# Causal attention of a four-layer kernel: heads taken in pairs, fp32 products in four groups of 32 columns, keys read from a DRAM scratch

## The chip, the cores and the metric

The kernel runs on one core of a Trainium2 chip. Its engines work side by side: TensorE (PE, with its weight loads as PEld), VectorE (DVE), ScalarE (ACT), GpSimd (POOL) and SyncE (SP), which here only issues DMAs. The metric is the device time of one launch in microseconds (us), the median of several runs.

## What is computed

The reference runs four layers, each a gated attention-like block and a gated feed-forward block, on x of 4 x 512 x 512. The change touches one block alone, the attention of layer 3: the queries are the normalised x, keys and values are both ctx_2048 (4 x 512 x 512), 16 heads of 32 columns, causal.

```python
qh = q.reshape(B, Sq, HEADS, hd).transpose(0, 2, 1, 3)      # B 4, Sq 512, HEADS 16, hd 32
scores = jnp.einsum('bhqd,bhkd->bhqk', qh, kh) / math.sqrt(hd)
scores = jnp.where(causal[None, None], scores, jnp.asarray(MASKED_BIAS, scores.dtype))
attn = jax.nn.softmax(scores, axis=-1)
out = jnp.einsum('bhqk,bhkd->bhqd', attn, vh)
...
x = x + jnp.tanh(g_xattn[3]) * _L3_xattn_ref(_layernorm(x, axis=-1), ctx_2048, ctx_2048)
```

## The kernel before

The whole program is a chain of stages with a barrier after each; only `layer3_xattn` (L2593) and its `attention_causal` (L2053) are touched. Two stages of it matter. `transposed_parts` (L174) normalises x, splits it into a high and a low fp16 part and turns both into `qT`; in this one use its SP queue also reads the same two parts of the context from a DRAM scratch, `context_parts`, into `kT` (L122, L123).

`attention_causal` then works on 64 items, one for each of 16 heads and 4 batches. N is 2048 = 4 batches of S = 512 rows, P = 128, KT = 4. An item has these steps:

- **Loading.** SP copies, head by head, six slices of 128 KB from `qT` and `kT` into `qs` and `ks` (L2103, L2104): the two fp16 parts stacked in 3 x 32 = 96 rows, so that one product gives a score from split operands.
- **Tops** (`score_for_top`, L2165, L2167). For 128, 256, 384 and 512 keys TensorE makes the scores of 128 queries each, and adds a causal mask by a second product; DVE takes the maximum of each (L2310) and splits the negated maximum into two fp16 numbers (L2314, L2316).
- **The turn of the shift.** TensorE turns those (L2176), ACT copies them out (L2256), and SP sends them by two DMAs into rows 96 and 97 of `qs` (L2117). In `ks` these rows hold the number 1024, and rows 98 to 127 of both were cleared by DVE at the start (L2354 to L2357), so that the second score product, over all 128 rows, comes out already less its maximum.
- **Scores and exponentials** (L2185, L2186, L2264), transposed: keys on partitions, 512, 384, 256 and 128 queries wide; ACT takes the exponential of three pieces.
- **Mix** (L2195). Four fp32 products of 64 columns (32 of the head's values, 32 ones, in `hv`, which POOL fills at L2138) with 512, 384, 256 and 128 moving columns give the numerator and the sums in one bank, `mixed_at`.
- **Evacuation.** DVE copies the sums (L2321), then ACT the numerator (L2272), and only then may the next mix begin. DVE inverts a 128 x 128 piece per item (L2324), POOL multiplies once a head (L2145), TensorE turns the head's output (L2202) and DVE adds it to x in four instructions (L2338).

Each engine's order is written out by hand. On TensorE one item is: tops of the item four further on, scores of the next item, mix of this item, turn of the shift. Loops of four heads on PE and two on ACT and DVE carry heads 2 to 13.

`attention_clipped` (L1497), the attention of layer 2, is not touched; it is named because it contains fp32 products of 32 columns (L1566, L1569) in four groups.

## Time and profile before

| | |
|---|---|
| Median of 3 runs | 4006.91 us (4003.19 to 4008.08) |
| The profiled execution | 4001.78 us, its span 4000.0 us |
| Engines busy in the span | PE 3024.1 us (76%), DVE 2748.0 (69%), ACT 1869.0 (47%), POOL 736.7 (18%) |
| Mean granted TensorE clock | 0.879 of full |

The profile is one execution: every time below is taken from it, with 0 at its first instruction. Shares of the whole span say little here, since the stages have different limits; `attention_causal` occupies the stretch from 3569.9 us to 3892.4 us. Matmuls are pipelined: a record runs on past the start of the next, so what a product costs is read from start to start. An fp32 product leaves two records, one for each of its passes, and a timeline row merges records that follow each other.

### The profile page before, as it was taken

How to read it: one execution, taken by the hardware profiler on the slowest of the kernel's cores; microseconds unless marked ns; L12 is line 12 of the kernel's file. 1: busy time of each engine (PE TensorE's matmuls, PEld its weight loads, DVE VectorE, ACT ScalarE, POOL GpSimd, SP SyncE). 2: the span in 40 equal slices, each digit the busy share in tenths (PEclk: the TensorE clock that was granted, in tenths of full speed). 3: DMA queues.
4: the chain of work that ended last, by engine and by line, in shares of the span. 5: the costliest groups of instructions: out<-in, count | busy, mean ns of one | idle time of the engine just before them, and what ended most of it. 6: DMA issues, size and time to landing. Idle time of an engine off the chain costs nothing. (4 is left out here: it accounts for less than half of the span.)

```text
span 4000.0 us, 66664 instructions
## 1 busy us (share of the span) xinstructions
PE 3024.1 (76%) x21656; PEld 1554.8 (39%) x21656; DVE 2748.0 (69%) x4984; ACT 1869.0 (47%) x2753; POOL 736.7 (18%) x595
## 2 busy tenths in 40 slices
PE   4999579977679999999965477867885137749972
PEld 2444334433346556565643233332112113225541
DVE  4322542326689999999965666443996877988877
ACT  2222422223259999999973333314770112425531
POOL 4222020001210000000022133120115002540102
PEclk9999679999789999999987688878997559969996
DMA  3000300010000000000003000102310200032201
GB/s 126 11 0 0 126 1 0 0 55 11 14 16 11 12 11 6 11 11 11 1 11 129 11 0 0 53 14 61 77 43 19 84 0 0 0 108 49 46 21 45
DMA packets 52277, 120.49 MB, mean 30 GB/s; under 512 B 11312, under 2 KB 14384, under 8 KB 50224
## 3 DMA queue, kind: packets, MB, share of 16 engines
q1 hardware_dynamic: 52144, 118.67, 10.0%
q8 instruction: 90, 1.47, 0.2%
q14 instruction: 43, 0.35, 0.0%
HBM read 72.37 MB, written 8.39 MB: 20 GB/s over the span
## 5 line engine op out<-in xcount | busy, mean ns | idle before, releaser
L1044 DVE TENSOR_REDUCE s_top<-ps 128x1 f32<-128x512 f32 x1024 | 657.0, 683 | 32.4 <-PE ps L939 32.0
L1013 ACT ACTIVATE s_prob<-ps,s_shift,m_sq 128x1024 int16<-128x1024 f32 x512 | 615.2, 1202 | 30.8 <-DVE s_shift L1052 30.8
L939 PE MATMUL ps<-s_ks,s_qs 128*128 128x512 f16 x1024 | 352.0, 386 | 61.6 <-issue 15.6
L944 PEld LDWEIGHTS ps<-ident,s_prob 128*128 128x128 f16 x4096 | 272.9, 98 | 123.5 <-DVE m_o L1062 51.7
L944 PE MATMUL ps<-ident,s_prob 128*128 128x128 f16 x4096 | 314.5, 220 | 0.7 <-ACT s_prob L1013 0.5
L932 PE MATMUL ps<-s_ks,s_qs 128*128 128x512 f16 x1024 | 307.3, 382 | 1.0 <-ACT s_prob L1013 0.5
L242 PE MATMUL ps<-ident,s_parts 128*128 128x128 f16 x1024 | 126.2, 300 | 217.2 <-POOL s_parts L233 214.7
L1019 ACT ACTIVATE s_probT<-ps 128x1024 f16<-128x1024 int16 x256 | 262.1, 1024 | 6.8 <-PE ps L944 6.3
L604 DVE SCALAR_TENSOR_TENSOR s_prod<-ps,scale,s_silu 128x512 f32<-128x512 f32 x64 | 48.0, 750 | 230.1 <-ACT s_silu L588 230.1
L376 DVE TENSOR_TENSOR s_prod<-ps,s_masked 128x512 f32<-128x512 f32 x64 | 44.3, 692 | 218.6 <-POOL s_masked L352 218.6
L242 PEld LDWEIGHTS ps<-ident,s_parts 128*128 128x128 f16 x1024 | 93.9, 136 | 251.8 <-POOL s_parts L233 251.8
L222 ACT ACTIVATE s_parts<-s_rows 128x512 f16<-128x512 f32 x112 | 69.4, 628 | 248.4 <-DVE s_rows L253 190.0
L317 PE MATMUL ps<-m_cT,s_hid 128*128 128x512 f16 x768 | 175.6, 379 | 9.6 <-DVE s_hid L371 9.6
L305 PE MATMUL ps<-m_hT,m_cT 128*128 x768 | 177.7, 383 | 1.9 <-PEq L104 1.9
L1057 DVE CAST s_probT<-ps 128x1024 f16<-128x1024 int16 x256 | 174.2, 681 | 3.2 <-PE ps L944 3.2
L1643 DVE TENSOR_SCALAR s_prob<-ps,s_cap 128x1024 f32<-128x1024 f32 x128 | 158.1, 1269 | 24.9 <-PE ps L1552 24.9
L588 ACT ACTIVATE s_silu<-ps,scale 128x512 f32<-128x512 f32 x64 | 44.0, 687 | 258.3 <-PE ps L556 258.3
L233 POOL TENSOR_TENSOR s_parts<-s_rows,s_parts 128x512 f16<-128x512 f32 x112 | 137.4, 1259 | 116.5 <-ACT s_parts L222 116.5
L1587 ACT ACTIVATE s_prob<-s_prob 128x1024 f32<-128x1024 f32 x128 | 131.1, 1051 | 58.3 <-DVE s_prob L1643 55.3
L923 POOL TENSOR_TENSOR s_sums<-s_z 128x16 f32<-128x16 f32 x16 | 3.5, 217 | 835.9 <-DVE m_o L1062 835.9
L340 ACT ACTIVATE s_silu<-ps 128x512 f32<-128x512 f32 x64 | 38.1, 596 | 249.2 <-PE ps L305 249.2
L2195 PE MATMUL ps<-s_prob,s_hv 128*64 128x512 f32 (+3 forms) x512 | 152.0, 440 | 3.0 <-ACT s_num L2272 2.9
(301 smaller groups left out, 6522.2 us busy)
## 6 DMA issues: line engine op xcount, KB each, us to landing
s_qs<-m_qT SPq DMA_DIRECT2D x144, 128.0 KB, 2.4
s_ks<-m_kT SPq DMA_DIRECT2D x144, 128.0 KB, 2.4
x_sb<-in_x SPq DMA_DIRECT2D x1, 4096.0 KB
s_rows<-in_ctx SPq DMA_DIRECT2D x16, 256.0 KB, 2.9
context_parts<-m_cT SPq DMA_DIRECT2D x1, 4096.0 KB, 17.2
m_nat<-in_L_ffn_W_up SPq DMA_DIRECT2D x4, 1024.0 KB, 9.6
m_nat<-in_L_ffn_W_gate SPq DMA_DIRECT2D x4, 1024.0 KB
m_nat<-in_L_ffn_W_down SPq DMA_DIRECT2D x4, 1024.0 KB, 6.6
```

The lines of the kernel that those rows point to most:

```text
L242: t = pe.transpose(k.ps16[:, u, cols(m, P)], parts[:, u, m // DC, cols(m % DC, P)], k.ident[:])
L305: i = pe.matmul(k.ps[:, n % A, :], cT[:, lw, c, e * D + f * P:e * D + (f + 1) * P], hT[:, lx, c, bass.ds(g * GT, GT)], start=(m == c == 0) ...
L317: i = pe.matmul(k.ps[:, YB + t, :], hid[:, n % Q, lh, cols(t, P)], cT[:, lw, f, cols(e, D)], start=(n == m == 0), stop=(n == UNITS - 1 and ...
L932: j = pe.matmul(pair(half)[:, m, :], qs[:, hb, bass.ds(t * P, P)], ks[:, hb, cols(2 * half + m, 512)], start=True, stop=True)
L939: pe.matmul(quarter_at(q), qs[:, hb, bass.ds(t * P, P)], ks[:, hb, cols(q, 512)], start=True, stop=True).then_inc(s.top_scored, 1)
L944: j = pe.transpose(turned(half, F16)[:, cols(m, P)], prob[:, u, cols(8 * half + m, P)].bitcast(F16), k.ident[:])
L1013: act.activation(prob[:, u, cols(half, HALF)], pair(half).rearrange("p m n -> p (m n)"), ACT.Exp, bias=shift[:, u:u + 1], scale=sq[:, bass ...
L1019: act.activation(probT[:, u, 8:16, :].rearrange("p m n -> p (m n)"), turned(1, I16), ACT.Copy).then_inc(s.half1_copied, 1)
L1044: dve.tensor_reduce(top4[:, u, q:q + 1], quarter_at(q), AX.X, ALU.max).then_inc(s.top_read, 1)
L1057: dve.tensor_copy(probT[:, u, 0:8, :].rearrange("p m n -> p (m n)"), turned(0, I16)).then_inc(s.half0_copied, 1)
L1643: dve.tensor_scalar(prob[:, n % R, :, :], k.ps[:, 2 * (n % A):2 * (n % A) + 2, :], cap[:, tile:tile + 1], -LIMIT, ALU.min, ALU.max).then_i ...
L2195: j = pe.matmul(mixed_at[0:2 * HD, t * P:S], hv[:, a, b * KT + t, :], prob[:, b % 2, START[t]:START[t] + S - t * P], start=(t == 0), stop= ...
```

## The change

`attention_causal` is rewritten for items of a pair of heads and a batch: 32 items instead of 64. What it does, with line numbers of the changed file:

- **Keys** come straight from the scratch into `ks`, 512 KB per DMA for four heads, three DMAs for each group of four heads (L2116). `kT` and the two reads in `transposed_parts` are gone. `ks` has eight head slots instead of four, `qs` four pairs. Queries still come from `qT`, in 128 KB DMAs whose pieces are now 1 KB long (L2110).
- **98 rows.** The score product contracts 98 rows, the tops 96 as before, so nothing is cleared. The rows of 1024 are written as fp32 words of two, in two instructions of 2 x 4096 (L2337, L2342).
- **Tops** of a pair: the same products and maxima for each head, the widest first; the two splitting instructions, the turn, the copy and the DMA of the shift are once for the pair. The turn goes to a spare part of bank 1.
- **Scores** use three banks in rotation, six pieces for an item.
- **Mix** (L2205): for each key tile four fp32 products of 32 columns, one for each group of 32 columns of TensorE: values of head 0, values of head 1, ones, ones. It is cut in three places of the item, after which the sequence returns to fp16 products.
- **Evacuation**: ACT copies both, 64 x 512 each (L2290, L2291). When four heads are together, for 16 outputs in all, TensorE multiplies the sums with a 128 x 4 picking matrix (L2216, four products), DVE inverts 128 x 16 numbers (L2326), TensorE turns the numerators (four fp32 transposes), DVE weighs them with gate and inverse in one instruction (L2332), and POOL adds to x.
- All loops are written out.

```diff
-            for m, (lq, lk) in enumerate(((0, 0), (1, 0), (0, 1))):
-                    sp.dma_start(qs[cols(m, HD), r, :], qT[cols(a, HD), lq, c, :]).then_inc(loaded[r], 16)
-                    sp.dma_start(ks[cols(m, HD), r, :], kT[cols(a, HD), lk, c, :]).then_inc(loaded[r], 16)
...
+            def load_queries(pair):
+                for j in range(2):
+                    head = 2 * pair + j
+                    for m, l in enumerate((0, 1, 0)):
+                        sp.dma_start(qs[cols(m, HD), pair % 4, :, j, :],
+                                     qT[cols(head % 4, HD), l, head // 4, :].rearrange("p (b n) -> p b n", b=B)
+                                     ).then_inc(q_loaded[pair % 4], 16)
+
+            def load_keys(c):
+                for m, l in enumerate((0, 0, 1)):
+                    sp.dma_start(ks[cols(m, HD), cols(c % 2, 4), :], context[:, :, l, c, :]).then_inc(k_loaded[c % 2], 16)
+
+            load_keys(0)
+            load_queries(0)
             sp.dma_start(ctx[:], k.ctx_in.rearrange("(t p) d -> p t d", p=P)).then_inc(s.ctx_loaded, 16)
+            load_queries(1)
+            load_keys(1)
+            load_queries(2)
+            for m in range(ITEMS):
+                pair, b = m // B, m % B
+                sp.wait_ge(s.shift_copied, m + 1)
+                sp.dma_start(qs[ROWS:ROWS + 2, pair % 4, b, :, :], shiftT[:, b, :]).then_inc(shifted[b], 16)
+                if b == 2 and 1 <= pair < PAIRS - 2:
+                    if pair >= 2:
+                        sp.wait_ge(s.scored, 6 * B * (pair - 1))
+                    load_queries(pair + 2)
+                    if pair % 2 and pair >= 3:
+                        load_keys(pair // 2 + 1)
...
+            def mix(m, t):
+                pair, b = m // B, m % B
+                if t == 0 and m:
+                    pe.wait_ge(s.evacuated, 2 * m)
+                pe.wait_ge(s.exp_ready, 6 * m + 2 * min(t, 2) + 2)
+                for rows, of in ((0, None), (2 * HD, ones)):
+                    for j in range(2):
+                        lhsT = ctx[:, b * KT + t, cols(2 * pair + j, HD)] if of is None else ones[:]
+                        i = pe.matmul(mixed_at[rows + j * HD:rows + (j + 1) * HD, t * P:S], lhsT,
+                                      prob[:, m % 2, j, START[t]:START[t] + S - t * P], start=(t == 0), stop=(t == KT - 1))
...
+            def turn_sums(i):
+                c, b = i // B, i % B
+                pe.wait_ge(s.evacuated, 2 * ((2 * c + 1) * B + b + 1))
+                if i:
+                    pe.wait_ge(s.weighed, i)
                 for q in range(KT):
+                    w = pe.matmul(turned_at[:, cols(q, 4)], sums[:, b, cols(q, P)], pick[:], start=True, stop=True)
+                w.then_inc(s.sums_turned, 1)
...
+            for m in range(B):
+                top(m, 0)
+                top(m, 1)
+                turn_shift(m)
+            pe.wait_ge(s.ones_set, 1)
+            for e in range(3):
+                for j in range(2):
+                    score(0, e, j)
+            pe.wait_ge(s.ctx_loaded, 16)
+            for m in range(ITEMS + 2):
+                after, ahead = m + 1 < ITEMS, m + B < ITEMS
+                if after:
+                    score(m + 1, 0, 0)
+                    score(m + 1, 0, 1)
+                if ahead:
+                    top(m + B, 0)
+                if out_of(m - 1) is not None:
+                    turn_sums(out_of(m - 1))
+                if m < ITEMS:
+                    mix(m, 0)
+                if after:
+                    score(m + 1, 1, 0)
+                    score(m + 1, 1, 1)
+                if m < ITEMS:
+                    mix(m, 1)
+                if ahead:
+                    top(m + B, 1)
+                if out_of(m - 1) is not None:
+                    turn_num(out_of(m - 1))
+                if after:
+                    score(m + 1, 2, 0)
+                    score(m + 1, 2, 1)
+                if m < ITEMS:
+                    mix(m, 2)
+                    mix(m, 3)
+                if ahead:
+                    turn_shift(m + B)
...
+            for m in range(-1, ITEMS):
+                for e in range(3):
+                    for j in range(2):
+                        if m + 1 < ITEMS:
+                            exp(m + 1, e, j)
+                if m >= 0:
+                    evacuate(m)
+                    if m + B < ITEMS:
+                        copy_shift(m + B)
...
+            for m in range(ITEMS + 2):
+                if m + B < ITEMS:
+                    tops(m + B, 0)
+                if out_of(m - 1) is not None:
+                    invert(out_of(m - 1))
+                if m + B < ITEMS:
+                    tops(m + B, 1)
+                    shifts(m + B)
+                if out_of(m - 1) is not None:
+                    weigh(out_of(m - 1))
...
-        kT = sb("kT", [P, 2, DC, N], F16)
         ctx = sb("ctx", [P, T, D], F32)
-        transposed_parts(k, qT, context=kT)
-        attention_causal(k, qT, kT, ctx, 3)
+        transposed_parts(k, qT)
+        attention_causal(k, qT, ctx, 3)
```

On TensorE, between the scores of one item and the tops of the next, one mix of an item stood before (ps is PSUM, s_prob the exponentials, s_hv values beside ones):

```order
L2186 MATMUL ps<-s_laterT,ident 128x128
L2195 MATMUL ps<-s_prob,s_hv 64x512
L2195 MATMUL ps<-s_prob,s_hv 64x384
L2195 MATMUL ps<-s_prob,s_hv 64x256
L2195 MATMUL ps<-s_prob,s_hv 64x128
L2176 MATMUL ps<-ident,s_shift 8x128
L2165 MATMUL ps<-s_ks,s_qs 128x128
```

Now, in an item that also finishes an output, the picking products (s_pick) and the first of the three pieces of the mix stand between tops and scores (m_ctx is the context in fp32, s_ones the ones):

```order
L2169 MATMUL ps<-s_ks,s_qs 128x384
L2171 MATMUL ps<-s_later,ident 128x128
L2216 MATMUL ps<-s_pick,s_sums 128x4 x4
L2205 MATMUL ps<-s_prob,m_ctx 32x512 x2
L2205 MATMUL ps<-s_prob,s_ones 32x512 x2
L2191 MATMUL ps<-s_qs,s_ks 128x384
L2194 MATMUL ps<-s_laterT,ident 128x128
```

The mix of 64 columns for one head has become groups of four times 32 columns for two heads, and fp16 products stand between its pieces.

On SP, in the middle of the stage, the six loads of one head stood between groups of eight DMAs of shifts (s_shiftT) before:

```order
L2117 DMA s_qs<-s_shiftT 1x4x128 x8
L2103 DMA s_qs<-m_qT 32x2048
L2104 DMA s_ks<-m_kT 32x2048
L2103 DMA s_qs<-m_qT 32x2048
L2104 DMA s_ks<-m_kT 32x2048
```

Now, at the third item of pair 3, and again of pair 5:

```order
L2127 DMA s_qs<-s_shiftT 2x8x128 x4
L2110 DMA s_qs<-m_qT 32x4x512 x6
L2116 DMA s_ks<-context_parts 32x4x2048 x3
L2127 DMA s_qs<-s_shiftT 2x8x128 x4
L2110 DMA s_qs<-m_qT 32x4x512 x6
```

The keys of four heads are asked for at once, behind the queries of a pair, and the first item that needs them has its tops two places of TensorE's sequence later.

## Rows read from the trace of the kernel before

**Rows 1.** Windows of the attention stage: its opening, then first to last mix.

```profile
core 0: us, PE busy (x) PEld busy (x) DVE busy (x) ACT busy (x) POOL busy (x), PEclk, DMA share, GB/s
3587.20:3605.00 17.80, 12.05 (x60) 6.63 (x60) 10.87 (x30) 3.25 (x9) 1.17 (x2) 0.50 0.51 108
3605.00:3877.30 272.30, 263.42 (x1589) 145.47 (x1588) 233.28 (x532) 137.28 (x311) 25.52 (x28) 1.00 0.17 37
```

**Rows 2.** Timeline of PE, one item: start us, us, engine, line, operation.

```profile
3649.99 0.22 PE L2176 MATMUL ps<-ident,s_shift 128*8 128x128 f16 x1
3650.14 0.23 PE L2165 MATMUL ps<-s_ks,s_qs 96*128 96x128 f16 x1
...
3650.94 0.38 PE L2185 MATMUL ps<-s_qs,s_ks 128*128 128x512 f16 x1
...
3651.80 2.37 PE L2195 MATMUL ps<-s_prob,s_hv 128*64 128x512 f32 x8
3654.10 0.22 PE L2176 MATMUL ps<-ident,s_shift 128*8 128x128 f16 x1
```

**Rows 3.** Timeline, maxima of an item, split and turn.

```profile
3704.13 1.68 DVE L2310 TENSOR_REDUCE s_ntop<-ps 128x1 f32<-128x128 f32 x4
...
3706.39 0.22 PE L2176 MATMUL ps<-ident,s_shift 128*8 128x128 f16 x1
```

**Rows 4.** Timeline of PE, turn of an output, and what follows.

```profile
3715.60 0.66 PE L2202 MATMUL ps<-ident,s_out 128*128 128x128 f32 x4 [0.36 <-ACT s_shiftT L2256]
...
3716.09 0.22 PE L2165 MATMUL ps<-s_ks,s_qs 96*128 96x128 f16 x1
```

**Rows 5.** Timeline of layer 2's attention: one group of four products and around it.

```profile
2901.42 0.62 PE L1566 MATMUL ps<-s_prob,m_values 128*32 128x512 f32 x2
...
2901.43 0.62 PE L1569 MATMUL ps<-s_prob,s_ones 128*32 128x512 f32 x2
...
2901.68 0.59 ACT L1595 ACTIVATE s_sums<-ps 64x512 f32<-64x512 f32 x1
2901.88 0.60 PE L1566 MATMUL ps<-s_prob,m_values 128*32 128x512 f32 x2
...
2902.42 0.60 PE L1552 MATMUL ps<-s_qs,s_ks 128*128 128x512 f16 x2
...
2902.95 0.62 PE L1566 MATMUL ps<-s_prob,m_values 128*32 128x512 f32 x2
```

**Rows 6.** Timeline, fp32 weight loads of 128 columns in the last stage.

```profile
3960.81 1.78 PEld L2410 LDWEIGHTS ps<-ident,s_ws_col 128*128 128x128 f32 x8 [2.80 <-DVE s_ws_col L2436]
```

**Rows 7.** Windows of 2 us: DRAM to SBUF (`kT`), then SBUF to SBUF.

```profile
3539.00:3541.00 2.00, 0.00 (x0) 0.00 (x0) 2.00 (x4) 0.00 (x0) 0.00 (x0) 0.50 1.00 375
...
3592.00:3594.00 2.00, 0.82 (x4) 0.23 (x2) 1.91 (x6) 0.00 (x0) 0.00 (x0) 0.50 1.01 211
```

**Rows 8.** Timeline of SP's queue (duration is the issue's).

```profile
3569.93 0.58 SPq L2103 DMA_DIRECT2D s_qs<-m_qT  x1
3570.56 0.58 SPq L2104 DMA_DIRECT2D s_ks<-m_kT  x1
```

**Rows 9.** Timeline, opening of the stage.

```profile
3580.30 6.88 DVE L2357 MEMSET s_ks<- 2x8192 f16 x1 [1.76 <-issue]
...
3587.29 0.26 PE L2165 MATMUL ps<-s_ks,s_qs 96*128 96x128 f16 x1 [18.91 <-DVE s_ks L2357]
...
3591.89 1.68 DVE L2310 TENSOR_REDUCE s_ntop<-ps 128x1 f32<-128x128 f32 x4 [1.00 <-PE ps L2167]
...
3594.98 1.69 DVE L2310 TENSOR_REDUCE s_ntop<-ps 128x1 f32<-128x128 f32 x4 [1.00 <-PE ps L2167]
```

**Rows 10.** Timeline, end of the stage.

```profile
3891.23 1.13 DVE L2338 SCALAR_TENSOR_TENSOR x_sb<-ps,gate,x_sb 128x128 f32<-128x128 f32 x4 [2.67 <-PE ps L2202]
```

**Rows 11.** Timeline of PE in `fp8_ffn`: the same products before and after idle time.

```profile
3489.60 1.51 PE L1966 MATMUL ps<-m_wproj,s_hid 128*128 128x512 f16 x4 [2.68 <-DVE s_hid L2038]
...
3494.75 1.03 PE L1966 MATMUL ps<-m_wproj,s_hid 128*128 128x512 f16 x4
```

401 lines of the change are left out of this document (146 added, 255 removed).

## The prediction

> **What bounds the kernel now.** I read the page first, which shows DVE and TensorE both busy and no bound for the whole, and then only the stage that changes, in windows. Between its first and its last mix, 272.3 us, TensorE is busy 263 us, DVE 233 and ACT 137, at the full clock of 2.4 GHz [rows 1]. So TensorE sets the pace. Its timeline confirms that: from one turn of the shift to the next, 3649.99 to 3654.10, an item takes 4.11 us with no wait of note, made of 0.15 us, the tops 0.80, the scores with the step to fp32 0.86 (some 0.77 for their columns and 0.09 for the step), and the mix, 2.30 until the next turn [rows 2]. The 63 intervals from 3605.0 to 3877.3 average 4.32 us, since every fourth item also turns an output. Two parts of the stage are not bound so: the opening, where TensorE stood until DVE had written the rows of 1024 at 3587.2 [rows 9], and the end.
>
> Everything below is a time within this stage, which ends at 3892.4 us [rows 10]. Nothing behind it is moved. The profiled execution took 4001.8 us, 5.1 us less than the median 4006.9; I carry a difference of the profiled times over to the median.
>
> **The grouped product.** The mix has 1280 moving columns. Four clocks of 2.4 GHz for each make 2.13 us, 0.85 us for 512, and leave 0.17 of the 2.30 us for the step back to fp16. The changed products are not in this stage, but their form is in layer 2: four products of 32 columns begin within 0.01 us of each other, the second passes follow 0.46 us later, the next fp16 product 1.00 us after the first, and two of these (0.43 us of columns) take until 0.53 us later [rows 5]. So four run side by side for the price of one, and each excursion costs 1.53 - 0.85 - 0.43 = 0.25 us. For a pair the mix becomes 2.13 + 3 x 0.25 + 0.07 for the fourth, narrow group = 2.95 us, where two items paid 2 x (2.30 + 0.09) = 4.78.
>
> A page speaks against taking the full factor. The Trainium skill, TensorE: Matmul & The Clock Gate, Part 3: Packing small matmuls, gives 2.38 times for three column tiles of 512 columns, not three. By it a group would cost 3 / 2.38 = 1.26 of one product, and an item 0.56 us more; an estimate from that page. The row of layer 2, 1.00 us for four with all its stepping, is the measured one here, and I take it; what the page's ratio would do is a rival below.
>
> **The rest of TensorE's item.** Tops 2 x 0.80, scores 2 x 0.77, the turn and step 0.15, all unchanged products: with the mix 6.24 us. The contraction over 98 rows instead of 128 I cost at nothing: the tops over 96 rows run at the same pace as the scores over 128 [rows 2]. A new wait comes at the turn. The second head's tops begin 2.3 us before it (0.80, scores 0.53, last mix groups 0.96), but its chain on DVE takes longer: the widest product and a hand-off 0.45, the maxima 1.68, and 0.58 from their end to the turn [rows 3], 2.7 in all. TensorE waits 0.4 us: 6.64 for a plain item.
>
> The evacuation, two copies of 0.59 us [rows 5] and three hand-offs of some 0.18 [rows 3], lasts 1.7 us from the end of a mix, and the next mix needs it. Those 0.4 us of waiting, the turn, two scores (0.53) and one head's tops (0.80) add up to 1.9 us, so it is covered; where tops are missing, at the end, it isn't.
>
> **Finishing an output.** Sixteen times four fp32 transposes at 0.49 us [rows 4], as before, and four picking products with 4 moving columns. For those only the weight loads count. No row has them at full clock: lower bound 0.5 us, as if like the four transposes; upper bound 1.8 us, the eight loads of 128 fp32 columns at half the clock under products of 128 columns [rows 6]. I take 1.1, since eight passes at the transposes' 0.12 us make 1.0. An item with an output has no wait at the turn, as the transposes stand before it: 6.24 + 1.1 + 0.5 = 7.84 us.
>
> **DVE, ACT and POOL** lose their share. DVE does 2 x 1.68 for the maxima, 0.5 for the split and at most 0.9 for an output out of 6.6 to 7.8 us; sums' copy, 128 x 128 inversion and four additions go. They hid under TensorE and give nothing by themselves. ACT is no bound either: its 137.3 us for 63 items [rows 1] are 4.4 us a pair, and its work hardly changes.
>
> **The opening.** DVE's three clearing instructions, the last ending at 3587.2 with the first product at 3587.29 [rows 9], go; the one that remains at the start writes half as many elements and ends by 3575. Late next are the loads. From the first issue at 3569.9 data flow from about 3571.3. DRAM to SBUF went at 375 GB/s, SBUF to SBUF at 211 [rows 7]. The first keys are 1.57 MB (4.2 us), the first queries 0.79 MB (3.7 us): first product at 3580, 7 us earlier. The 1 KB pieces of the queries are not in the trace; I take the rate of the 4 KB pieces, with half of it as the other bound. Then four pairs of tops instead of four single ones: a round on DVE took 3.09 us (3591.89 to 3594.98), of which 1.68 the maxima [rows 9]; a pair takes 2 x 1.68 + 1.41 = 4.8 us, four 19.1. That is over at 3599. But the first shift can only land behind all that SP has asked for before it: 7.3 MB from DRAM (19.6 us) and 2.4 MB of queries (11.2), until 3602 or 3603. Before, TensorE reached its first mix at 3605.0. Now six score pieces at half the clock last until 3606.1, and the first item pays 1.3 us more for its slow start. The seven microseconds gained are given back, for twice the tops done ahead.
>
> **The keys in the middle.** Keys for pairs 4 and 5 are asked for once the shift of item 14 is copied, 1.7 us into the item before the one that needs them. SP issues one DMA each 0.63 us [rows 8]: the shift, six of queries, then keys at 6.1 to 7.4 us. The queries' data take 3.7 us and the keys' 4.2, so they land near 11.7 us. TensorE wants them 0.7 us into the next item, at 7.3. It stands 4.4 us, with scores and mixes queued behind; the same with the keys of pair 6. After 2.7 us of idle time the same four products took 1.51 us instead of 1.03 [rows 11]; I add 2 us for the slower clock. Twice 6.5 makes 13 us.
>
> **The sum.** 28 items run ahead: 16 plain (106.2) and 12 with an output (94.1). The last four have no tops, and stand for the evacuation: 5.6, 7.2, 7.2 and 5.9 us; the last output adds 6.4 (evacuation 1.7, picking 1.1, transposes 0.5, three wide instructions and hand-offs 3.1): 32.3. Together 3606.1 + 1.3 + 200.3 + 13 + 32.3 = 3853.0 against 3892.4: 39.4 us less, 3962 for the profiled execution and 3968 as the median.
>
> **Rivals.**
> - The keys land in time: if SP runs further ahead or the queries' data go faster, 13 us are gone: 3955. For it: keys come from DRAM at the better rate. Against: the count of issues alone, nine of them, takes 5.7 us.
> - The queries in 1 KB pieces go at half the rate: 11 us more at the opening and 3.7 at each of two stalls: 3986. The page's 2.38 for three tiles would cost 32 x 0.56 = 18 us by the sentence above, and ends at the same 3986; the row of layer 2 speaks against it.
> - A group can't go below the 0.46 us a pass that layer 2 shows, whatever its width, because four weight loads stand under it. All rows there are 512 wide, so they can't exclude it. Eight passes would be 3.68 us, the item 1.3 longer, 42 us in all: 4009, no change.
> - Slower: only two of the four products run side by side, because here the values are read with a stride and the widths differ within an item. Then the columns cost double: 2.13 x 32 = 68 us, 4036. It decides from 39.4 / 32 = 1.2 us more an item. Against it stand starts 0.01 us apart with the same arrangement.
>
> **Chances.** Forecast 0.56, keys in time 0.17, slower queries or the page's ratio 0.12, a floor for each pass 0.10, two at a time 0.05. A difference of 0.2%, 8 us, is what a measurement can tell. The first three are faster, 0.85; the floor counts as the same, 0.10; slower 0.05. The likeliest case's own range: picking products 10 us down or 11 up, excursions 0.1 us cheaper or dearer, 10 either way: 3950 to 3986. With keys in time below it and part of the floor above: 3937 to 4000.
>
> **What would show it.** Right: items 6.6 and 7.8 us apart on TensorE at full clock; four L2205 records starting together; two gaps of 4 to 5 us before L2169 that wait for a DMA; the stage some 283 us instead of 322.5; DVE busy about 60% of it. A wait at L2176 for DVE of 0.4 us. Wrong, if L2205's narrow groups stay at 0.46 us a pass, if L2216 takes over 2 us, if the first score waits well past 3603, or if the mix waits for ACT's copies each time.

## The result, and the profile after

| | median, us | ratio to before, 95% interval | stage, us |
|---|---|---|---|
| before | 4006.5 (4003.2 to 4008.1) | | 323.3 |
| changed | 3978.8 (3976.7 to 3982.2) | 0.9933, 0.9915 to 0.9950 | 296.4 |

The change makes the kernel 0.67% faster, 27.7 us by the medians. 3968 was forecast, 39.4 us less. The right-hand column is what most of the following goes by: the time from SP's first request of the attention stage to its first request of the stage behind it (L396), in the profiled execution. It leaves out the rest of the program, which differs by some microseconds from one execution to the next: the stage began at 3569.93 us before, at 3571.87 after, and anywhere from 3569.6 to 3575.3 us in the runs below. Ahead of it only the two reads into `kT` are gone, in `transposed_parts`, and that gained nothing: from ACT's last instruction of the stage ahead of that one (L1988, at 3519.43 and 3521.47 us) to SP's first request here it is 50.5 us before and 50.4 after. The profiled execution after took 3976.9 us, its span is 3975.1.

Windows of the changed stage: opening to first mix, then 27 items up to the last turn of a shift, then the end. The columns are those of [rows 1].

```profile
core 0: us, PE busy (x) PEld busy (x) DVE busy (x) ACT busy (x) POOL busy (x), PEclk, DMA share, GB/s
3571.87:3615.12 43.25, 19.03 (x97) 9.70 (x97) 22.08 (x44) 6.35 (x13) 1.15 (x7) 0.50 0.88 225
3615.12:3836.18 221.06, 193.79 (x1954) 102.38 (x1952) 114.07 (x304) 112.25 (x248) 15.17 (x12) 0.95 0.15 34
3836.18:3867.31 31.13, 24.53 (x225) 12.48 (x225) 4.04 (x8) 14.20 (x29) 5.06 (x4) 0.89 0.01 1
```

Where TensorE was busy for 263 of 272 us [rows 1], it is now busy for 194 of 221, and DVE, 233 us before, has fallen to 114. The granted clock, 1.00 before, is 0.95 here and 0.89 at the end; the rows below show where TensorE stood.

TensorE's timeline, the turns of the shift at the end of two plain items and of two with an output; they answer to [rows 2]. The number in brackets is idle time before the row and who ended it.

```profile
3639.76 0.22 PE L2176 MATMUL ps<-ident,s_shift 128*16 128x128 f16 x1 [0.31 <-DVE s_shift L2321]
...
3646.32 0.22 PE L2176 MATMUL ps<-ident,s_shift 128*16 128x128 f16 x1 [0.31 <-DVE s_shift L2321]
...
3669.73 0.22 PE L2176 MATMUL ps<-ident,s_shift 128*16 128x128 f16 x1
...
3677.68 0.22 PE L2176 MATMUL ps<-ident,s_shift 128*16 128x128 f16 x1
```

A plain item takes 6.56 us with a wait of 0.31 for DVE at its turn, an output item 7.95 without one. Two items of before took 8.22 us for the same work.

The narrow groups of one mix, then the picking products of an output ("x2" or "x8" is the number of records in the row).

```profile
3690.05 0.41 PE L2205 MATMUL ps<-s_prob,m_ctx 128*32 128x256 f32 x2
3690.06 0.41 PE L2205 MATMUL ps<-s_prob,s_ones 128*32 128x256 f32 x2
...
3690.28 0.39 PE L2205 MATMUL ps<-s_prob,m_ctx 128*32 128x256 f32 x2
...
3690.50 0.28 PE L2205 MATMUL ps<-s_prob,m_ctx 128*32 128x128 f32 x2
...
3690.61 0.28 PE L2205 MATMUL ps<-s_prob,m_ctx 128*32 128x128 f32 x2
...
3716.19 1.00 PE L2216 MATMUL ps<-s_pick,s_sums 128*128 128x4 f32 x8
```

Pass after pass the numerators' and the sums' products start within 0.02 us of each other, 0.23 us apart at 256 columns, 0.11 at 128. The eight picking passes take 0.93 us to the next product, the four transposes (not shown) 0.44.

The opening, in SP's queue and TensorE's, with windows beside it, of the first keys and queries and then of the values; it answers to [rows 7] and [rows 9].

```profile
3571.87 1.28 SPq L2116 DMA_DIRECT2D s_ks<-context_parts  x3
...
3578.19 12.59 SPq L2110 DMA_DIRECT2D s_qs<-m_qT  x6
...
3585.37 0.58 PE L2169 MATMUL ps<-s_ks,s_qs 96*128 96x512 f16 x1 [14.99 <-DMA s_qs<-m_qT]
...
3598.34 1.40 SPq L2127 DMA_DIRECT2D s_qs<-s_shiftT  x2
...
3609.66 0.59 PE L2191 MATMUL ps<-s_qs,s_ks 98*128 98x512 f16 x1 [5.44 <-DMA s_qs<-s_shiftT]
...
3573.00:3584.50 11.50, 0.00 (x0) 0.00 (x0) 3.27 (x1) 0.16 (x1) 0.11 (x1) 0.50 1.02 220
3586.00:3588.00 2.00, 2.00 (x14) 1.11 (x13) 1.90 (x5) 0.00 (x0) 0.00 (x0) 0.50 1.05 388
```

The first product starts 13.5 us after the first request and the first score 37.8. While keys and queries are under way the 16 DMA engines are full (share 1.02) and yet move 220 GB/s; the values, right behind them, go at 388. SP's queue is held up too: six requests take it 12.59 us, and the first shift, which ACT has copied at 3590.42, is asked for only at 3598.34. The first score starts 11.3 us after that request.

The first of the two stops in the middle: SP's requests, TensorE's first product behind the gap, and windows.

```profile
3693.01 3.87 SPq L2110 DMA_DIRECT2D s_qs<-m_qT  x6
...
3696.92 1.55 SPq L2116 DMA_DIRECT2D s_ks<-context_parts  x3
...
3707.28 0.58 PE L2169 MATMUL ps<-s_ks,s_qs 96*128 96x512 f16 x1 [8.63 <-issue]
...
3698.00:3700.00 2.00, 0.66 (x4) 0.20 (x4) 0.00 (x0) 1.82 (x5) 0.00 (x0) 1.00 0.82 176
3700.00:3702.00 2.00, 0.00 (x0) 0.00 (x0) 0.00 (x0) 0.00 (x0) 0.00 (x0) 0.55 1.04 223
...
3706.00:3707.00 1.00, 0.00 (x0) 0.00 (x0) 0.00 (x0) 0.00 (x0) 0.00 (x0) 0.50 0.04 8
```

The keys were asked for at 3696.92, behind six requests for queries. TensorE wanted them at 3698.66 and began 8.63 us later; "issue" means that the wait's end is not one that the trace names, but what is in flight then is the keys, at 176 to 223 GB/s, and e2 below shows that the wait goes with them. The data are through by about 3705.7; from 3706 on next to nothing moves (8 GB/s), and the product starts 1.5 us or so behind the last data. The clock falls to half, and the products that follow take 0.58 us instead of 0.38. From turn to turn this item takes 16.80 us and the other such item 18.67, against 6.56: the two stops cost 10.2 and 12.1 us.

The end of the stage: the last turn, windows 2 us long, and POOL's last addition, answering to [rows 10].

```profile
3836.18 0.22 PE L2176 MATMUL ps<-ident,s_shift 128*16 128x128 f16 x1 [0.31 <-DVE s_shift L2321]
...
3842.00:3844.00 2.00, 1.62 (x12) 1.13 (x16) 0.26 (x1) 1.41 (x3) 0.00 (x0) 0.89 0.00 0
3844.00:3846.00 2.00, 2.00 (x12) 0.39 (x4) 0.00 (x0) 0.25 (x1) 0.00 (x0) 0.50 0.00 0
...
3866.05 1.26 POOL L2152 TENSOR_TENSOR x_sb<-x_sb,s_y 128x512 f32<-128x512 f32 x1 [3.37 <-DVE s_y L2332]
```

From the last turn to POOL's end the four items without tops take 31.1 us. Inside, the clock falls to half for one of the windows.

### The profile page after: what moved, and what is told of

The parts are those of the page before. It is cut to its first block and busy times, and to the rows that moved or that the text cites. A ratio compares the mean times of both kernels' runs of the same rounds, so it can differ in the third digit from the quotient of the medians.

```text
span 3975.1 us, 66295 instructions
## 1 busy us (share of the span) xinstructions
PE 2982.5 (75%) x22264; PEld 1524.8 (38%) x22264; DVE 2623.7 (66%) x4759; ACT 1859.2 (47%) x2721; POOL 727.1 (18%) x581
## 5 line engine op out<-in xcount | busy, mean ns | idle before, releaser
L1044 DVE TENSOR_REDUCE s_top<-ps 128x1 f32<-128x512 f32 x1024 | 657.3, 684 | 31.1 <-PE ps L939 30.5
L2311 DVE TENSOR_REDUCE s_ntop<-ps 128x1 f32<-128x512 f32 (+3 forms) x256 | 107.5, 484 | 122.1 <-PE ps L2171 122.1
L317 PE MATMUL ps<-m_cT,s_hid 128*128 128x512 f16 x768 | 177.3, 382 | 10.7 <-DVE s_hid L371 10.7
```

The source lines that it names most:

```text
L317: i = pe.matmul(k.ps[:, YB + t, :], hid[:, n % Q, lh, cols(t, P)], cT[:, lw, f, cols(e, D)], start=(n == m == 0), stop=(n == UNITS - 1 and ...
L1044: dve.tensor_reduce(top4[:, u, q:q + 1], quarter_at(q), AX.X, ALU.max).then_inc(s.top_read, 1)
```

## The experiments

All are edits of the changed kernel, and each ratio is to runs of the kernel before taken beside it. e4 and e11 are single runs, read for their traces and not for their time.

| run | median, us | ratio to before, 95% interval | stage, us |
|---|---|---|---|
| e1_keys_first | 3966.0 | 0.9898, 0.9881 to 0.9914 | 288.0 |
| e2_keys_early | 3951.4 | 0.9863, 0.9847 to 0.9880 | 272.4 |
| e3_shifts_first | 3971.6 | 0.9910, 0.9894 to 0.9927 | 290.2 |
| e4_rates | 3986.2, one run | | |
| e5_two_tiles | 4041.3 | 1.0091, 1.0075 to 1.0108 | 359.0 |
| e6_rows128 | 3976.6 | 0.9931, 0.9914 to 0.9947 | 295.5 |
| e7_all_loads | 3945.4 | 0.9856, 0.9840 to 0.9873 | 262.4 |
| e8_lead_three | 3947.7 | 0.9858, 0.9842 to 0.9875 | 264.6 |
| e9_top_earlier | 3946.3 | 0.9853, 0.9838 to 0.9868 | 263.3 |
| e10_three_deferred | 3945.1 | 0.9846, 0.9833 to 0.9860 | 262.2 |
| e11_two_queues | 3942.3, one run | | 263.8 |
| e12_changed_again | 3977.2 | 0.9933, 0.9917 to 0.9948 | 292.9 |

The changed kernel gave 296.4 us in one profiled execution and 292.9 in the other (e12). The rows of the two differ in two places only, the two stops (35.5 and 33.6 us for their items) and the end (32.1 and 30.5 us); the items between agree to 0.01 us. So a difference of 2 us in the stage says something only where the rows show its place.

### Is it the requests or the bytes that make the keys late?

```diff
                     if b == 2 and 1 <= pair < PAIRS - 2:
...
-                    load_queries(pair + 2)
                     if pair % 2 and pair >= 3:
                         load_keys(pair // 2 + 1)
+                    load_queries(pair + 2)
```

> The same requests at the same place, but at items 14 and 22 the three requests for keys stand before the six for queries. Theory (bytes): the keys are 1.57 MB that go to 32 partitions at a time at some 210 GB/s, 7.5 us instead of the 4.2 us of the forecast, and they stand behind 3.7 us of queries. Then going first gives back 3.7 us of data and about 1 us of issues: both stalls at L2169 fall from 8.6 and 9.3 us to about 4 us but stay, and with the slower clock behind them the time falls by about 10 us against the changed kernel, to about 3969 us. Rival (issues): nine requests at 0.65 us each and a fixed landing time set the stall. Then three requests alone are out after 2 us, the stalls go to 0.5 us or nothing, and the time falls by some 20 us to 3958.

SP's requests and the first product behind the stop in e1:

```profile
3694.58 1.36 SPq L2116 DMA_DIRECT2D s_ks<-context_parts  x3
3695.98 4.00 SPq L2110 DMA_DIRECT2D s_qs<-m_qT  x6
...
3704.55 0.58 PE L2169 MATMUL ps<-s_ks,s_qs 96*128 96x512 f16 x1 [4.33 <-issue]
```

The keys are asked for first, and their consumer still starts 10.0 us after the request. The two waits are 4.33 and 4.17 us (8.63 and 9.31 before), and the two items take 13.15 and 13.20 us. The theory of the bytes said about 4, that of the requests 0.5 or nothing. The time is 3 us below what the bytes' theory gave. The bytes decide: 1.57 MB of keys need 7 to 8 us, not 4.2. The rest of the 10.0 us is some 0.9 us from the request to its first data and, as in the first stop above, 1.5 us behind the last.

### What do the two stops cost in all?

```diff
                     load_queries(pair + 2)
-                    if pair % 2 and pair >= 3:
+                    if pair % 2 == 0:
+                        sp.wait_ge(s.scored, 6 * B * pair)
                         load_keys(pair // 2 + 1)
```

> The keys for pairs 4 and 6 are asked for at items 10 and 18, one pair earlier than in the changed kernel, when the buffer of four heads that they go into has been read. Every theory of the stall has both waits at L2169 gone here, since the data have more than 20 us. What is told apart is what the two stalls cost in all: if it is the 22.4 us read from the intervals (10.2 and 12.1 over 6.56), the time is about 3956 us; if part of them is only a wait that DVE's and ACT's backlog would have cost anyway, or if the transfer beside running items slows them, it is 3960 to 3968 us. Items around 10 and 18 stay at 6.6 and 7.9 us if a transfer beside TensorE costs nothing.

The turns around the item that stood before, in e2:

```profile
3695.95 0.22 PE L2177 MATMUL ps<-ident,s_shift 128*16 128x128 f16 x1 [0.31 <-DVE s_shift L2322]
...
3702.50 0.22 PE L2177 MATMUL ps<-ident,s_shift 128*16 128x128 f16 x1 [0.31 <-DVE s_shift L2322]
```

No wait for a DMA is left in the middle; this item takes 6.55 us, as its neighbours do, also while the transfer runs. The stage is 24.0 us shorter (20.5 against e12), the time 27 us by the medians. The stops' 22.4 us and 1.7 us in the end of the stage make up the 24.0; in e12 the stops cost 20.4 us, which is the 20.5. What the medians have beyond that lies outside the stage, where this change does nothing, so I read it as spread. The prediction's 3955 for "keys in time" is 4 us off.

### The opening: is the shift late because of what stands ahead of it?

```diff
             load_queries(1)
-            load_keys(1)
-            load_queries(2)
             for m in range(ITEMS):
...
                 sp.dma_start(qs[ROWS:ROWS + 2, pair % 4, b, :, :], shiftT[:, b, :]).then_inc(shifted[b], 16)
+                if m == 3:
+                    load_keys(1)
+                    load_queries(2)
```

> Only the opening changes: keys of heads 4 to 7 and queries of pair 2, 2.4 MB that nobody needs before item 4, are asked for behind the first four shifts and not before them. Theory: the first score waited 5.4 us for its shift because the shift stood behind all 9.4 MB. Then the first score starts about 5 us earlier, 32.5 us after the stage's first request instead of 37.8, nothing else moves, and the time is about 3974 us. Rival: the first score waits for the shift's own path (turn, copy, a request with a fixed landing time of some 2 us), or something else comes late next (the values of the context, needed by the first mix): then less than 2 us are gained, 3977 to 3979.

The last turn of the opening and the first score in e3:

```profile
3605.49 0.27 PE L2177 MATMUL ps<-ident,s_shift 128*16 128x128 f16 x1 [1.31 <-DVE s_shift L2322]
3605.69 0.61 PE L2192 MATMUL ps<-s_qs,s_ks 98*128 98x512 f16 x1
```

The first score follows 0.20 us behind the turn with no wait, 31.9 us after the stage's first request instead of 37.8. From there to the next turn it takes 10.19 us instead of 16.14: 5.95 us, and 7 by the medians. Nothing else came late, so the shift had waited behind the requests and the data ahead of it. How much of the wait was SP's queue and how much the data is not told apart by this run.

### What rate do keys really get, and why?

```diff
+            sp.wait_ge(s.scored, 6 * ITEMS)
+            sp.dma_start(ks[0:HD, 4:8, :], context[:, :, 0, 3, :]).then_inc(k_loaded[1], 16)
+            sp.wait_ge(k_loaded[1], 112)
+            sp.dma_start(ks[HD:2 * HD, 4:8, :], context[:, :, 0, 3, :]).then_inc(k_loaded[1], 16)
+            sp.dma_start(ks[0:HD, 4:8, :], context[:, :, 0, 3, :]).then_inc(k_loaded[1], 16)
+            sp.dma_start(ks[2 * HD:3 * HD, 4:8, :], context[:, :, 1, 3, :]).then_inc(k_loaded[1], 16)
+            sp.wait_ge(k_loaded[1], 160)
+            sp.dma_start(ks[:, 4, :], k.context_parts[:, 0:N]).then_inc(k_loaded[1], 16)
+            sp.wait_ge(k_loaded[1], 176)
+            sp.dma_start(ks[:, 5, :], k.context_parts[:, N:2 * N]).then_inc(k_loaded[1], 16)
+            sp.dma_start(ks[:, 6, :], k.context_parts[:, 2 * N:3 * N]).then_inc(k_loaded[1], 16)
+            sp.dma_start(ks[:, 7, :], k.context_parts[:, 3 * N:4 * N]).then_inc(k_loaded[1], 16)
+            sp.wait_ge(k_loaded[1], 224)
```

> A measurement of transfer rates: the changed kernel, and behind its last score eight more transfers of 512 KB each from the same scratch into key buffers that are no longer read, in rows of 4 KB: one alone into partitions 0 to 31; three together into partitions 0 to 95, 32 each; one alone over 128 partitions; three together over 128 partitions. Theory: it is the 32 partitions of the target that set the rate, so the first and the three go at 210 to 246 GB/s (three in 6.4 to 7.5 us) and those over 128 partitions at 375 GB/s (three in 4.2 us). Rival (queues): the rate in the changed kernel was low because the keys shared the engines with queries; then all of them go at 375 GB/s here. Second rival (source): the scratch or the shape is slow whatever the target; then all go at 210 to 246.

Windows in e4, first of the three transfers into 32 partitions each, then of the three over 128 (the last two columns are the share of the DMA engines and GB/s), and what SP waited for:

```profile
3859.50:3864.50 5.00, 2.17 (x12) 1.68 (x12) 1.01 (x2) 0.69 (x2) 1.63 (x2) 0.72 1.04 235
3872.50:3875.50 3.00, 0.00 (x0) 0.00 (x0) 0.00 (x0) 0.00 (x0) 0.00 (x0) 0.50 1.01 410
...
SPq L2141 <- DMA s_ks<-context_parts: 8.4, 1, 8.4
SPq L93 <- DMA s_ks<-context_parts: 4.8, 1, 4.8
```

The engines are full in both, and move 235 GB/s in the one and 410 in the other. The source, the length of a row (4 KB) and the amount are the same, and no queries are under way, so both rivals fall: it is the form of the transfer, 32 partitions at a time. SP's waits tell the same in time: 8.4 us from the last of three requests until the data are there, against 4.8.

The Trainium skill, SBUF — State Buffer, Door 1: The DMA port swizzle, says this in a table: partitions 0 to 31 reach 8 of the 16 ports, and a transfer into them tends to some 218 GB/s, one over 128 partitions to 436. The measured rates, 235 and 410 GB/s, agree within 8%; the first lies above the table's figure, and the measurement decides. By the first, as an estimate, the keys of four heads take 7.2 us and the first keys and queries together (2.36 MB) 10.8; the trace of the changed kernel has them under way from 3573 to 3584.5 us, 11.5, at 220 GB/s. This rule of the Trainium skill would have put the prediction's term right; the prediction took its rate from a load over 128 partitions instead.

### Two at a time instead of four

```diff
                     for j in range(2):
-                        i = pe.matmul(mixed_at[rows + j * HD:rows + (j + 1) * HD, t * P:S], lhsT,
+                        i = pe.matmul(mixed_at[j * HD:(j + 1) * HD, t * P:S], lhsT,
...
-                                      prob[:, m % 2, j, START[t]:START[t] + S - t * P], start=(t == 0), stop=(t == KT - 1))
+                                      prob[:, m % 2, j, START[t]:START[t] + S - t * P], start=(t == 0 and of is None),
+                                      stop=(t == KT - 1 and of is not None))
```

> The changed kernel with its four products of a group in two column tiles instead of four: the sums' two go to the tiles of the numerators and are added onto them, so the output is not the attention (the sums' rows are never written), while instructions, operands and columns are the same. Theory (the gain hangs on four running side by side at the price of one): a group now costs double, 2.13 us more an item less the 0.3 us of waiting at the turn that it covers, so plain items go from 6.56 to about 8.4 us and output items from 7.95 to about 10.1, 32 items cost some 62 us, and the time is about 4041 us, slower than the kernel before. Rival (most of an item's mix is fixed: weight loads, excursions, hand-offs): then an item grows by 1 us at most, and the time is below 4011.

Two turns of plain items, and a group of its mix, in e5:

```profile
3631.79 0.22 PE L2176 MATMUL ps<-ident,s_shift 128*16 128x128 f16 x1
...
3639.09 0.62 PE L2205 MATMUL ps<-s_prob,m_ctx 128*32 128x256 f32 x4
3639.55 0.60 PE L2205 MATMUL ps<-s_prob,s_ones 128*32 128x256 f32 x4
...
3640.42 0.22 PE L2176 MATMUL ps<-ident,s_shift 128*16 128x128 f16 x1
```

Plain items take 8.62 us and output items 10.05, and the sums' products now start 0.46 us behind the numerators' where they had started together. The stage is 62.6 us longer and the time 4041.3 us, as forecast (4041). The kernel leaves out the writing of the sums' own rows, so its output is not the attention, but instructions and columns are the same. With two tiles instead of four more than the gain is gone: it is slower than the kernel before. The prediction's fourth rival had this mechanism and gave it 4036.

### The number of rows

```diff
+            sp.wait_ge(s.cleared, 1)
...
+            pool.memset(qs[ROWS:P, :, :, :, :].bitcast(F32), 0.0).then_inc(s.cleared, 1)
+            pool.wait_ge(s.cleared, 1)
+            pool.memset(ks[ROWS:P, 4:8, :].bitcast(F32), 0.0).then_inc(s.cleared, 1)
...
-                    pe.matmul(at, ks[0:ROWS + 2, a, b * S + t * P:b * S + (t + 1) * P],
-                              qs[0:ROWS + 2, pair % 4, b, j, t * P:S],
+                    pe.matmul(at, ks[:, a, b * S + t * P:b * S + (t + 1) * P],
+                              qs[:, pair % 4, b, j, t * P:S],
...
+            dve.memset(ks[ROWS:P, 0:4, :].bitcast(F32), 0.0).then_inc(s.ks_cleared, 1)
+            dve.wait_ge(s.ks_cleared, 1)
             dve.memset(ks[ROWS:ROWS + 2, 0:4, :].bitcast(F32), TWO_ONES).then_inc(s.ones_set, 1)
```

> The changed kernel, but its score products contract over all 128 rows, as before the change, with rows 98 to 127 cleared (keys of the first four heads on DVE, the rest on POOL). Theory: the number of rows costs nothing, so items stay at 6.56 and 7.95 us, and as both DVE and POOL are idle while the first loads are under way, the clearing hides too: 3977 to 3980 us. Rival (a product or its weight load is cheaper over 98 rows): the LDW of L2191 is longer than 100 ns or its items longer than 6.56 us; 0.1 us an item would make 3982. Second rival (the clearing was what the change saved in the opening): the first product or the first score starts later than 13.5 and 37.8 us after the stage's first request.

Two turns of plain items in e6:

```profile
3635.70 0.22 PE L2182 MATMUL ps<-ident,s_shift 128*16 128x128 f16 x1 [0.34 <-DVE s_shift L2327]
...
3642.24 0.22 PE L2182 MATMUL ps<-ident,s_shift 128*16 128x128 f16 x1 [0.33 <-DVE s_shift L2327]
```

6.54 us an item with 128 rows, 6.56 with 98; the first turn of the shift comes 17.9 us after the first request against 18.0, and the first turn behind the opening 48.2 us after it in both. Ratio 0.9931 against 0.9933. The rows cost nothing, and neither does clearing them where the loads cover it.

### All loads moved

```diff
+            def load_half(half, sem):
+                for m, l in enumerate((0, 0, 1)):
+                    sp.dma_start(ks[cols(m, HD), cols(half, 2), :], context[:, cols(half, 2), l, 0, :]).then_inc(sem, 16)
...
-            load_keys(0)
+            load_half(0, s.first_keys)
             load_queries(0)
             sp.dma_start(ctx[:], k.ctx_in.rearrange("(t p) d -> p t d", p=P)).then_inc(s.ctx_loaded, 16)
+            load_half(1, k_loaded[0])
             load_queries(1)
```

with the edits of e2 and e3; TensorE's first top waits for the semaphore `first_keys`.

> Loads only: keys one pair earlier as in the second run, first shifts ahead of the keys of heads 4 to 7 and of the queries of pair 2 as in the third, and new: of the first keys only those of heads 0 and 1 (0.79 MB) stand before the first queries, those of heads 2 and 3 behind the values. Theory (bytes set the opening): 0.79 MB at 210 GB/s is 3.7 us, so the first product starts 9.8 us after the stage's first request instead of 13.5, and all of the opening with it, as the four rounds of maxima take 18.8 us from there. Sum from the changed kernel: 22.4 + 6.0 + 3.7 = 32 us by the intervals of the traces, 3947; by the medians of the earlier runs (27 + 7 + 3.7) 3941. Rival: the values, 4.2 MB, land later than the first mix needs them once the rest is earlier, or the first request's own landing sets the start: then 2 us or less of the 3.7 come, 3943 to 3949.

The first product in e7:

```profile
3572.99 1.28 SPq L2120 DMA_DIRECT2D s_ks<-context_parts  x3
...
3582.57 0.59 PE L2176 MATMUL ps<-s_ks,s_qs 96*128 96x512 f16 x1 [11.07 <-DMA s_qs<-m_qT]
```

It starts 9.6 us after the first request instead of 13.5, 3.9 us earlier; 0.79 MB at some 210 GB/s take 3.8. The stage is 34 us shorter than in the first trace of the changed kernel and 30.5 than in e12; 32 was the sum. All three terms came, and none was given back. The time, 3945.4 us, is within the 3941 to 3947 of the theory, and 1.4% below the kernel before.

### Three items of lead instead of four

```diff
+    LEAD = 3
...
-            for m in range(B):
+            for m in range(LEAD):
                 top(m, 0)
...
-                    top(m + B, 0)
+                    top(m + LEAD, 0)
...
-                if b == 2 and 1 <= pair < PAIRS - 2:
+                if b in (1, 2) and 1 <= pair < PAIRS - 2:
...
-                    load_queries(pair + 2)
+                    load_queries(pair + 2, (b - 1,))
+                if 11 <= m <= 13 or 19 <= m <= 21:
+                    c = 2 if m < 16 else 3
+                    sp.wait_ge(s.scored, 12 * B * (c - 1))
+                    load_keys(c, (m % 8 - 3,))
```

and so on DVE and ACT.

> As the run before it, and the maxima run three items ahead instead of four, so that the opening has three rounds on DVE instead of four and the end three items without tops instead of four; and because a shift now has one item to land in, queries are asked for by head at items 1 and 2 of a pair and the keys in three requests at three items. Theory: one round of 4.7 us goes from the opening, one item of 7.2 us at the end becomes one of 7.0 to 7.9 that works ahead, items otherwise stay at 6.56 and 7.95 us: about 4.5 us less than the run before it, some 3937 to 3942. Rival (the shift lands late): a request that stands behind 0.5 MB of keys needs 1.3 us of issues, 2.5 us of data and its own 2 us, near the 6 us it has; if it is late, the first score of items 12 to 14 and 20 to 22 waits for its DMA, up to 2 us each, and the gain is gone or below zero.

What TensorE waited for in e8, in us, times and the longest (of the waits for a DMA):

```profile
PE ps L2179 <- DMA s_qs<-m_qT: 11.2, 1, 11.2
PE ps L2201 <- DMA s_qs<-s_shiftT: 3.6, 1, 3.6
```

The forecast failed. The round of 4.7 us went, but 4.0 of it came back at once: the first score now waits 3.6 us for its shift, for which SP's other data are in the way again, as e10 confirms. The rival's waits at items 12 to 14 and 20 to 22 did not come. And the end gave less than I had counted: one more item at 6.56 us against 3.8 less behind the last turn (26.4 instead of 30.2), since the items without tops are short ones, not 7.2. Sum: -4.7 + 4.0 + 6.6 - 3.8 = 2.1 us more; the stage is 2.2 longer.

### The wait at the turn

```diff
                 if m < ITEMS:
                     mix(m, 0)
+                if ahead:
+                    top(m + B, 1)
...
                     mix(m, 1)
-                if ahead:
-                    top(m + B, 1)
```

on top of e7.

> As the run with all loads moved, and in each item the second head's tops stand ahead of the second scores, before the mix of tile 1 and not behind it. Theory (the wait of 0.31 us at the turn is DVE's chain from the second head's tops): the chain starts some 1.3 us earlier, the wait at L2176's place is gone from the 16 plain items, they take 6.24 us and not 6.56, and the stage gets 5 us shorter: 257.4 us from its first request to the next stage's, against 262.4; the time is about 3940 us. Items with an output stay at 7.95. Rival (the wait moves): DVE has not yet read the first head's widest top when the second head's wants its bank, or ACT's exponentials come late for the scores, and items stay at 6.5 us.

Two turns (L2183 here), and two of TensorE's waits at the tops (L2176 here), in e9:

```profile
3625.53 0.22 PE L2183 MATMUL ps<-ident,s_shift 128*16 128x128 f16 x1
...
3632.07 0.22 PE L2183 MATMUL ps<-ident,s_shift 128*16 128x128 f16 x1
...
PE ps L2176 <- DVE s_ntop L2318: 5.5, 12, 0.5
PE ps L2176 <- ACT s_shiftT L2281: 4.8, 15, 0.3
```

The wait at the turn is gone, as the theory had it, and the item is 6.53 us instead of 6.56. TensorE waits 0.3 us a little later, where a top needs the bank of the shift that ACT copies behind its two evacuations; the output items now wait 0.5 for the maxima and take 8.00 instead of 7.95. So the rival was right that the wait moves, though to ACT, which it did not name for this. The work of an item without waits comes to 6.53 - 0.3 = 6.2 us.

### Three of lead, with the loads deferred

```diff
             sp.dma_start(ctx[:], k.ctx_in.rearrange("(t p) d -> p t d", p=P)).then_inc(s.ctx_loaded, 16)
-            load_half(1, k_loaded[0])
-            load_queries(1)
...
+                if m == 0:
+                    load_half(1, k_loaded[0])
+                    load_queries(1)
                 if m == LEAD - 1:
                     load_keys(1)
```

on top of e8, with the order of e9.

> As the run with three items of lead, with the same order of tops as the run above, and keys of heads 2 and 3 and queries of pair 1 asked for behind the first shift. Theory: the 3.6 us for which the first score waited there stood behind 7.4 us of data that nobody needed yet, and go; with 5 us from the order of the tops the stage falls from 264.6 to 256 us, and the time to about 3939 us. Rival: pair 1's keys or queries are late for its first tops, 10 us behind the third turn, and the wait stands there (L2176's tops for a DMA), 2 to 4 us, so that the stage is 258 to 260.

The first score has no wait any more, and the stretch from the last turn of the opening to the next is 11.9 us instead of 14.3. But the other 5 us were e9's and were not to be had. The stage, 262.2 us, is e7's within what two executions differ, and so is the time.

### Two queues

```diff
-            load_half(0, s.first_keys)
-            load_queries(0)
+            first_loads(sp, 0)
+            first_loads(sp, 2)
...
+            first_loads(act, 1)
             act.preload_act_table(ACT.Exp)
```

`first_loads(engine, m)` asks for the keys and the queries of partitions 32m to 32m + 31 of pair 0; e7 otherwise.

> As the run with all loads moved, but the first keys and queries are asked for from two engines: those of partitions 0 to 31 and 64 to 95 by SP, those of 32 to 63 by ACT, so that transfers into different partitions are under way together. Theory (a transfer into 32 partitions is held up at its target): two at a time go at more than 300 GB/s while both have keys, and the first product starts 8 to 9 us after the first request instead of 9.8 to 10. Rival (what is slow is the row of 4 KB, the scratch or the SBUF source, whatever the target): the rate stays at 210 to 250 GB/s and the first product at 9.8 us.

The first product, and a window ahead of it, in e11:

```profile
3573.00:3575.00 2.00, 0.00 (x0) 0.00 (x0) 0.99 (x1) 0.00 (x0) 0.00 (x0) 0.50 1.07 201
3575.00:3577.00 2.00, 0.00 (x0) 0.00 (x0) 0.00 (x0) 0.00 (x0) 0.00 (x0) 0.50 1.11 220
...
3580.30 0.58 PE L2185 MATMUL ps<-s_ks,s_qs 96*128 96x512 f16 x1 [12.20 <-DMA s_qs<-m_qT]
```

Asked for by two engines, the transfers go at 201 to 220 GB/s together, and the first product starts 10.7 us after the first request, 1.1 later than in e7. So the theory's more than 300 GB/s did not come. SP asked for partitions 0 to 31 and ACT for 32 to 63 at once, and SP for 64 to 95 only 1.8 us later, behind its own first three; whether 64 to 95 ever went beside another target can't be read here, so the run excludes a gain for the first pair of targets and leaves it open for others. The Trainium skill (SBUF — State Buffer, "Can I just issue two DMAs to hit both halves?") answers no; the trace agrees as far as it goes. What e4 shows is that the rate goes with the width of the single transfer; why it does is not shown by these runs. Whether one request over 96 or 128 partitions would give the keys 390 GB/s was not tried.

### The changed kernel again

> The changed kernel itself again, beside the three above on one chip, since the medians of the stages before this one differ by some 2 us from call to call: 3975 to 3982 us, and the stage 296.4 us from its first request to the next stage's, within 1 us. Theory and rivals expect the same.

3977.2 us and a ratio of 0.9933, as the first time. The stage was 3.5 us shorter than before, more than the 1 us that I had allowed; the places stand above.

## The prediction, point by point

**The grouped product was right**, in the size that layer 2 gave [rows 5]. Plain items were forecast at 6.64 us and took 6.56, output items 7.84 and 7.95; the 27 intervals between the first and the last turn, without the two stops, took 193.8 us where the sum had 193.7. The factor of four holds at every width: 0.45 us a pass at 512, 0.23 at 256, 0.11 at 128. That fells the rival of the floor (0.46 us whatever the width, 4009 us), and e5 shows what two at a time would have cost. The 2.38 of the Trainium skill for three tiles, by which the sum would have been 18 us more, does not describe this kernel: four tiles started within 0.02 us of each other, and a group took the columns of one product.

**The small terms** came out close. Picking: 1.1 forecast, 0.93 measured, between the bounds of 0.5 and 1.8. Transposes: 0.5 and 0.44. The wait at the turn: 0.4 and 0.31, for DVE as said. Rows in the contraction: nothing and nothing (e6). The end: 32.3 and 31.1. DVE, forecast busy about 60% of the stage, was so for 52% of the window of the items, 57% without the stops.

**The keys in the middle: the mechanism was right, and the term mis-sized.** "Twice 6.5 makes 13 us" stands against 22.4 measured. The wait was to be 4.4 us a stop and was 8.6 and 9.3; the slow clock behind it was to cost 2 and cost 1.6 and 2.8. The step that failed is the one before: "The queries' data take 3.7 us and the keys' 4.2". The 4.2 was 1.57 MB at 375 GB/s [rows 7]. That row is a load of `kT` over 128 partitions, and the new keys go into 32 at a time; e4 measures 235 GB/s for that form and 410 for the other. At 210 the keys take 7.5 us, 3.3 more. e1 confirms it: with the keys in front, 4.2 to 4.3 us of waiting remain. The other 1 us or so has its place in the trace of the first stop: data flowed from about 3693.8 to 3705.7 us, 11.9 us for queries and keys where the sum had 7.9, beginning 1.2 us earlier than it put them, and 1.5 us passed between the last data and the product, for which it had no term.

**The opening failed by the same number.** The first product was to start 10.1 us after the first request and started 13.5 after it; 3.3 of the 3.4 us are the first keys' rate. The four rounds were right (19.1 forecast, 18.6 measured). The first shift was to land after 32.6 us, "behind all that SP has asked for before it", and came after 37.8: again the mechanism was right (e3: what stands ahead of the shift delays it), and the 3.15 MB of keys in front of it took about 14 us, by the 220 GB/s of the window above, not 8.4. "The seven microseconds gained are given back" was too mild: the first mix came 43.3 us after the first request, where it had come 35.1 us after it before. One of the prediction's own signs of being wrong, a first score well past 3603, did show: counted from the same start it is 3607.7.

**The balance of the stage.** Forecast 283.1, measured 295.4, to POOL's last addition: opening and first item 48.2 for 44.1, items 193.8 for 193.7, stops 22.4 for 13, end 31.1 for 32.3. The forecast of 39.4 us became 27.0 in the stage and 27.7 in the medians. Of the 12.3 us missed, the rate of the keys makes up 2 x 3.3 in the stops and, by the paragraph above, the 4.1 of the opening; the other 2.8 us of the stops are landing and slow clock, and the end gives 1.2 back. In e12 the stops cost 20.4 us instead of 22.4. The median of 3979 lies inside the range of 3950 to 3986, but that range was made of picking products and excursions and had no room set aside for a rate; that it held is luck.

**The rivals.** Keys in time (3955): no, the stops came; e2 shows what it would have been, 3951. Queries at half their rate (3986): no; those of pair 3, alone under way from 3636.5 to 3638 us, went at 206 GB/s, where 211 was assumed. The time of 3979 lies near that rival's 3986, but for another reason: it was the keys that were slow, and they were the transfer that the prediction held for safe ("keys come from DRAM at the better rate"). The uncertainty was put on the queries' 1 KB pieces, because no row showed them, while the row for the keys was taken as if it fitted.

**Theory by theory in the experiments**: the bytes (e1, e3, e4, e7) held each time; my attempts at TensorE's own schedule (e8, e9, and e10, which was to take both gains) failed, because a wait that is removed here has another 0.3 to 4 us behind it, and in e8 also because the items at the end are shorter than I had counted. In e11 the theory failed. The version that beats both kernels is the one with the loads moved: e7, 3945.4 us; e8, e9 and e10 (3945.1 us, ratio 0.9846, 0.9833 to 0.9860) can't be told apart from it.

## What to carry to other kernels

A bandwidth read from a row belongs to the form of that transfer: before carrying it over, compare how many partitions one request covers, not only the bytes and whether DRAM or SBUF is the source. When a stage is made faster on its leading engine, put the transfers next to it: ask for a buffer as soon as it is free (e2), and hold back what nobody needs yet when something urgent stands behind it (e3, e7): here the order of the requests was worth 31 to 34 us, more than the whole change had brought. And fp32 products with 32 output columns each shared TensorE four at a time at every width tried, 512 down to 128 moving columns, each writing a column tile of its own.

## What the runs showed of the hardware

- Six transfers of 512 KB from the same scratch in rows of 4 KB: three into 32 partitions each at 235 GB/s, three over 128 partitions at 410, with the DMA engines full in both. Two issuing engines did not raise the rate of transfers into 32 partitions (e11, 201 to 220 GB/s).
- Four fp32 products in four column tiles took 0.45, 0.35, 0.23 and 0.11 us a pass for 512, 384, 256 and 128 columns, 2.28 us for both passes of all four widths, where one product of each width took 2.30 before [rows 2]. In two tiles a group of 256 columns took 0.89 us instead of 0.45 (e5).
- Behind the first stop's keys about 1.5 us passed between the last data and the product that waited for them. In the opening six requests of 128 KB held SP's queue for 12.59 us, and the request for the first shift, nine requests behind those, went out 7.9 us after its data were ready.
- The changed kernel's end took 32.1 us in one execution and 30.5 in the other. In the first the granted clock was 0.50 in the window from 3844 to 3846 us, behind 2 us in which TensorE was busy for 1.6; in the other it was 1.00 in each of four windows around that place.
